# Attention scores computed by four row tiles of two heads instead of two row tiles of four heads, in a cross-attention and mixture-of-experts kernel

## The chip, the core and the metric

The kernel runs on one core of one Trainium2 chip. The metric is the device time of one execution in microseconds (us); lower is better. The core has TensorE (matrix products, written PE in the profile, its weight loads PEld), VectorE (DVE), ScalarE (ACT), GpSimd (POOL), and SyncE (SP), which issues most transfers. The engines run side by side, each takes its own instructions in order, and they meet by semaphores, which the kernel sets and waits for by hand.

## The reference, cut to what matters

All is f32. There are 4 sequences of 512 tokens of 256 features, and 64 context tokens for each sequence.

```
x1 = x + Wo( softmax( Q(layernorm(x)) K(ctx)^T / sqrt(16) ) V(ctx) ) + bo      # 16 heads of 16 features, 64 keys
gates = layernorm(x1) @ router_w + router_b ; the best 2 of 8 experts, softmax of their gates
out = x1 + mean over 2 shared experts of gelu(h @ sw1 + sb1) @ sw2 + sb2 + the 2 chosen experts, weighted
```

The change touches the term Q K^T alone: for each token 16 heads x 64 keys = 1024 scores.

## The kernel before

**Tiles and stages.** The 2048 tokens are 16 token tiles of 128 (NT = 16). Attention is a software pipeline over stages s. In one stage each engine works on several token tiles: the scores of tile s+1, maximum and shift of tile s, sums of tile s-1, transposes of tile s-2, values of tile s-3, output product of tile s-4, and the transposes of normalized rows of tile s-8. From stage 16 on, the products of the shared experts are interleaved with the rest of it (hidden products, line 1237, and output products, line 1143). After stage 47 come the routed experts. The order on each engine is written out by hand, and a wait holds up all that is behind it on its engine.

**What each engine issues in a stage of the attention.** Names are used below in this short form:

- TensorE: scores(s+1) (line 1084), then from s = 8 x2T(s-8) (line 1175), from s = 4 att(s-4) (line 1186), ot(s-3) (line 1198), tr(s-2) (eight transposes, line 1211), and in the odd stages 1 to 11 the query projection of two token tiles, q((s+3)/2) (line 1065).
- ScalarE: in the even stages QT, the copy of these queries from PSUM (line 549), then x2T(s-8) copy (line 600), OT(s-3) copy (line 607), exp(s) (line 612), rows(s-7) (line 618), PT(s-2) copy (line 624), and in stages 3 to 10 a copy of shared weights, s_hi (line 571). In stage 14 a copy xt_hi (line 577) follows.
- VectorE: max(s) (line 894, waits for scores(s)), shift(s) (line 903), in stages 0 to 8 statistics of x (lines 743 and 747), x1(s-4) (line 911, waits for att(s-4)), sum(s-1) (line 914, waits for exp(s-1)), statistics of x1 (line 920), reciprocal(s-1) (line 925).
- GpSimd: the product of the exponentials with the reciprocals (line 473), and small work.

**PSUM.** There are eight banks of 512 f32 columns. Scores have four, as two buffers of two banks (psS): token tile t takes buffer t % 2, and scores(t) waits until shift(t-2) has read its predecessor (line 1080). The bank psD serves q and att: att(s-4) waits until ScalarE has copied the queries out (qt_sb, line 1182), and q waits for x1 (line 1215). The bank psA serves x2T and ot: ot waits for the copy of x2T of the stage before (line 1194).

**Scores.** K is laid out as Kbd, block-diagonal: on the 64 partitions of a row tile lie 4 heads of 16 features, and each head has 64 columns of its own, zero on the partitions of the others. One product has 64 rows of Q (the stationary operand, 128 tokens) and 256 columns of Kbd. A token tile needs C = 2 chunks x RT = 2 row tiles = 4 products, which the trace shows as 8 instructions, since an f32 product is two instructions. The two row tiles write two different banks. Kbd is written by one VectorE product (batch 0, line 753) and HPR = 4 ScalarE copies (line 558), with masks that GpSimd makes (line 364).

Of the kernel before, what the change touches and what calls it, by code (L numbers as in the profile page):

```python
# [14 lines left out]
P = 128  # L15
# [4 lines left out]
L = 64  # L20
# [3 lines left out]
RT = 2  # L24
HPR = 4
# [87 lines left out]
def program(nc, ios, keep, scratch):  # L113
# [4 lines left out]
    with ExitStack() as es:  # L118
# [30 lines left out]
        psS = es.enter_context(nc.psum_tensor("psS", [P, 2, RT, 512], F32))  # L149
# [65 lines left out]
        def heads(t):  # L215

            return t.rearrange("p r (h k) -> p (r h) k", k=L)
# [127 lines left out]
        def _(pool):  # L345
# [18 lines left out]
            pool.tensor_tensor(out=maskK[:], in0=mask8[:, 0:HPR], in1=mask8[:, HPR:2 * HPR], op=ALU.add).then_inc(masks, 1)  # L364
# [173 lines left out]
        def _(act):  # L538
# [16 lines left out]
            act.wait_ge(masks, 11)  # L555
# [181 lines left out]
        def _(dve):  # L737
# [14 lines left out]
            dve.wait_ge(masks, 11)  # L752
# [137 lines left out]
            for s in range(FIRST_CHUNK + CHUNKS):  # L890
                if s < NT:
                    dve.wait_ge(scores_done, s + 1)
                    v = heads(psS[:, s % 2])
                    V.reduce_max(mx[:, s % 2], v, axis=AX.X).then_inc(max_done, 1)
# [4 lines left out]
                if s < NT:  # L899
                    if s >= NPR:  # L900
                        dve.wait_ge(pt_psum, s - NPR + 1)
                    dve.wait_ge(max_done, s + 1)
                    V.tensor_tensor(out=Pr[:, s % NPR], in0=v, in1=mx[:, s % 2].unsqueeze(2).to_broadcast([P, NH, L]),  # L903
                                    op=ALU.subtract).then_inc(shift_done, 1)
# [138 lines left out]
        def _(pe):  # L1043
# [25 lines left out]
            def scores(t):  # L1069
                b = t // TPB  # L1070
                if t == 0:
                    pe.wait_ge(q0_sb, 1)
                else:
                    pe.wait_ge(qt_sb, t // 2 + 1)
                if b == 0:
                    pe.wait_ge(k0_done, 1)
                else:
                    pe.wait_ge(k_done, HPR)
                if t >= 2:
                    pe.wait_ge(shift_done, t - 1)  # L1080
                for c in range(C):
                    for r in range(RT):
                        own = slice(r * L, (r + 1) * L)
                        last = T.matmul(psS[:, t % 2, r, c * HPR * L:(c + 1) * HPR * L], QT[own, t // 2 % 2, c, t % 2 * P:(t % 2 + 1) * P],  # L1084
                                        Kbd[own, c, b].rearrange("p h k -> p (h k)"), start=True, stop=True)
                last.then_inc(scores_done, 1)
# [9 lines left out]
            scores(0)  # L1096
            scores(1)
            queries(1)
            scores(2)

            pe.wait_ge(ld_wv, 16)
            for i, bank in enumerate((psA[:, :], psP[:, 1])):
                for b in range(2 * i, 2 * i + 2):
# [63 lines left out]
            for s in range(FIRST_CHUNK + CHUNKS):  # L1167
                if 2 <= s < NT - 1:
                    scores(s + 1)
# [7 lines left out]
                if 4 <= s < NT + 4:  # L1177
# [9 lines left out]
                    last.then_inc(att_psum, 1)  # L1187
                if 3 <= s < NT + 3:
# [6 lines left out]
                    for c in range(C):  # L1195
                        for j in range(TPB):
                            own = slice(CT * j, CT * (j + 1))
                            last = T.matmul(psA[own, D + c * P:D + (c + 1) * P], Vbd[:, t // TPB, c * P + CT * j:c * P + CT * (j + 1)],  # L1198
                                            PT[:, t % 2, 4 * (j // 2) + 2 * c + j % 2], start=True, stop=True)
# [23 lines left out]
                if 0 <= n < CHUNKS:  # L1223
                    q, e, k = n // CPG, n % CPG // HC, n % HC
                    if n == 0:
                        pe.wait_ge(shift_done, NT - 1)
# [143 lines left out]
def build(nc, a, out):  # L1370
    xg_d = nc.dram_tensor("xg_d", [XG_ROWS, ROW], F32, kind="Internal").ap()
    with ExitStack() as es:
# [13 lines left out]
        with ExitStack() as first:  # L1386
# [20 lines left out]
            Kbd, Vbd, QT = lay("Kbd", [P, C, B, HPR, L]), lay("Vbd", [P, B, D]), lay("QT", [P, 2, C, QT_TOK])  # L1407
            OT, WoT, bo_bc, sb2_bc = lay("OT", [P, 2, C, P]), lay("WoT", [P, C, D]), lay("bo_bc", [P, D]), lay("sb2_bc", [P, NSH, D])
# [63 lines left out]
```

## Time and profile before

| | us |
|---|---|
| median of 3 runs | 336.03 |
| the runs | 334.66, 340.51, 336.03 |
| the profiled execution | 332.25 |
| its span from first to last instruction | 330.5 |

| engine | busy share of the span |
|---|---|
| PE (matmul) | 93% |
| PEld (weight load) | 81% |
| DVE | 68% |
| ACT | 66% |
| POOL | 57% |

The trace is one execution. Times in its rows count from the start of its span. A row of the timeline gives start, duration, engine, line, operation, output<-input, shapes (partitions x elements) and count; a bracket at its end is the time that the engine sat idle before it, and what released it. Where several instructions are merged in a row (x8), the duration is from the first start to the last end; the next row can begin before that end, as matmuls are pipelined, so the time that a group takes from its engine is read from start to start.

### The profile page before, as it was taken

To read this page: it belongs to the slowest core of one execution; us is meant where nothing else is said; L and a number is where in the kernel's file an instruction comes from. 1 tells how busy PE (TensorE), PEld (TensorE's weight loads), DVE (VectorE), ACT (ScalarE), POOL (GpSimd) and SP (SyncE) were. 2 spreads that over 40 slices of the span, in tenths; PEclk is the share of its full clock that TensorE was granted. 3 is DMA by queue.
4 is the path that set the end of the run, shared out by engine and by line. 5 is a ranking of instruction groups with operands and counts; after the bars stand their busy time and mean duration, and the time that the engine had idled before them with its cause. 6 is when DMAs were issued, how large, how long until landed. Compare 5 with 4: busy or idle time off the path is not lost.

```text
span 330.5 us, 7676 instructions
## 1 busy us (share of the span) xinstructions
PE 307.7 (93%) x2390; PEld 269.0 (81%) x2390; DVE 225.2 (68%) x474; ACT 216.9 (66%) x438; POOL 189.0 (57%) x227
## 2 busy tenths in 40 slices
PE   3999999998899899999999999999999999999980
PEld 2767676676667787899999998989999999999970
DVE  0699999889815466688766546667687666667530
ACT  1365776777785886674855747667698678678540
POOL 5459889879943276676710071323355558557653
PEclk9999999999799999999999999999999999999995
DMA  7980000044000754245954704545447356544343
GB/s 245 401 330 2 3 0 3 0 129 177 16 18 1 269 195 147 97 153 143 319 192 127 216 8 119 93 71 93 65 83 97 64 99 98 74 57 52 47 52 44
DMA packets 27766, 36.32 MB, mean 110 GB/s; under 512 B 8368, under 2 KB 22064, under 8 KB 27344
## 3 DMA queue, kind: packets, MB, share of 16 engines
q1 hardware_dynamic: 19984, 25.02, 24.5%
q0 software_dynamic: 7456, 10.04, 17.8%
q10 hardware_dynamic: 288, 0.79, 0.8%
q8 instruction: 20, 0.33, 0.4%
q14 instruction: 18, 0.15, 0.2%
HBM read 22.64 MB, written 13.19 MB: 108 GB/s over the span
## 4 chain that ended last, share of the span: by engine, by line
PE 80%; ACT 6%; issue 4%; DVE 4%; DMA 3%; POOL 2%; SPq 0%; POOLq 0%; DVEq 0%; ACTq 0%
PE psS L1282 13%; PE psS L1237 12%; PE psP L1298 8%; PE psS L1143 4%; PE psP L1143 4%; PE psP L1302 4%; PE psD L1065 4%; PE psS L1329 4%; PE psS L1084 4%; PE psP L1211 3%; PE psP L1353 3%; PE psS L1146 2%; PE psP L1146 2%; PE psD L1186 2%; PE psA L1198 2%
## 5 line engine op out<-in xcount | busy, mean ns | idle before, releaser
L512 POOL DMA_INDIRECT out<-xres,meta x39 | 66.0, 1691 | 36.1 <-DMA out<-xres,meta 21.7
L936 DVE TENSOR_TENSOR h_lo<-g,h_hi 128x512 fp32r<-128x512 f32 x32 | 22.8, 713 | 33.8 <-ACT g L641 33.7
L640 ACT ACTIVATE h_hi<-psS,sb1T 128x512 fp32r<-128x512 f32 x32 | 22.0, 689 | 32.6 <-PE psS L1237 32.6
L473 POOL TENSOR_TENSOR Pr<-Pr,inv 128x1024 f32<-128x1024 f32 x16 | 31.3, 1956 | 11.5 <-DVE inv L925 11.5
L725 ACT ACTIVATE s_hi<-psS,b1c 128x256 fp32r<-128x256 f32 x60 | 25.6, 489 | 14.5 <-PE psS L1282 14.5
L1298 PE MATMUL psP<-w_lo,s_hi 128*128 x120 | 29.8, 281 | 0.0
L1298 PE MATMUL psP<-w_hi,s_hi 128*128 x120 | 29.7, 280 | 0.0
L1033 DVE TENSOR_TENSOR s_lo<-sraw,s_hi 128x512 fp32r<-128x512 f32 x30 | 20.6, 688 | 12.8 <-ACT sraw L728 12.8
L728 ACT ACTIVATE sraw<-psS,b1c 128x256 f32<-128x256 f32 x60 | 25.9, 502 | 0.0
L1237 PE MATMUL psS<-xt_hi,s_lo 128*128 128x512 f32 x64 | 25.4, 397 | 0.0
L1237 PE MATMUL psS<-xt_lo,s_hi 128*128 128x512 f32 x64 | 25.3, 395 | 0.0
L1237 PE MATMUL psS<-xt_hi,s_hi 128*128 128x512 f32 x64 | 25.0, 390 | 0.0
L1298 PEld LDWEIGHTS psP<-w_hi,s_hi 128*128 128x128 f32 x120 | 22.7, 189 | 0.0
L1298 PEld LDWEIGHTS psP<-w_lo,s_hi 128*128 128x128 f32 x120 | 22.7, 189 | 0.0
L641 ACT ACTIVATE g<-psS,sb1T 128x512 f32<-128x512 f32 x32 | 21.8, 682 | 0.0
L443 POOL DMA_INDIRECT xg_d<-rows_b,slots x16 | 18.4, 1153 | 5.9 <-issue 4.3
L443 POOL DMA_INDIRECT xg_d<-rows_a,slots x16 | 16.9, 1059 | 8.4 <-issue 4.3
L786 DVE TENSOR_TENSOR w_lo<-wraw,w_hi 128x512 fp32r<-128x512 f32 x32 | 20.9, 684 | 0.0
L503 POOL TENSOR_TENSOR s_free<-s_free,sbh 128x256 f32<-128x256 f32 x8 | 6.5, 849 | 25.0 <-DMA s_free<-in_b 25.0
L989 DVE SCALAR_TENSOR_TENSOR xres<-psP,meta,xres 128x256 f32<-128x256 f32 x26 | 12.6, 483 | 11.0 <-PE psP L1302 6.5
L903 DVE TENSOR_TENSOR Pr<-psS,mx 128x1024 f32<-128x1024 f32 x16 | 19.6, 1225 | 0.5
L1302 PE MATMUL psP<-w_hi,s_lo 128*128 x120 | 19.4, 284 | 0.0
(244 smaller groups left out, 1015.1 us busy)
## 6 DMA issues: line engine op xcount, KB each, us to landing
wraw<-in_w SPq DMA_DIRECT2D x16, 512.0 KB, 5.9
xg<-xg_d SPq DMA_DIRECT2D x15, 256.0 KB, 2.7
sraw<-in_sw SPq DMA_DIRECT2D x2, 1024.0 KB, 11.6
out<-xres SPq DMA_DIRECT2D x4, 512.0 KB, 3.2
xres<-in_x SPq DMA_DIRECT2D x3, 512.0 KB, 7.5
xTs<-in_xT SPq DMA_DIRECT2D x3, 512.0 KB, 8.4
xg<-xg_d SPq DMA_DIRECT2D x9, 128.0 KB, 2.1
xg_d<-filler SPq DMA_DIRECT2D x8, 130.0 KB, 2.2
```

Of the source, the lines that this page charges most:

```text
L443: pool.indirect_dma_start(xg_d, bass.IndirectOffsetOnAxis(ap=slots[:, k, t:t + 1], axis=0), row(t), None).then_inc(scattered[t // HALF_T][ ...
L473: pool.tensor_tensor(out=Pr[:, t % NPR], in0=Pr[:, t % NPR], in1=inv[:, t % 2].unsqueeze(2).to_broadcast([P, NH, L]), op=ALU.mult).then_in ...
L512: pool.indirect_dma_start(out, bass.IndirectOffsetOnAxis(ap=meta[:, n, 0:1].bitcast(U32), axis=0), y[:, n % NYB], None, compute_op=ALU.add ...
L640: A.activation(h_hi[:, n % 2], h_bank[n % 2], ACT.Gelu, bias=bias).then_inc(hhi_done, 1)
L725: ins = A.activation(hp_hi[:, i % 2, k], hp_bank[i % 2][k], ACT.Gelu, bias=b1c[:, i % 2, k:k + 1])
L728: ins = A.activation(gp[:, i % 2, k], hp_bank[i % 2][k], ACT.Gelu, bias=b1c[:, i % 2, k:k + 1])
L936: V.tensor_tensor(out=h_lo[:, n % 2], in0=g[:, n % 2], in1=h_hi[:, n % 2].bitcast(F32), op=ALU.subtract).then_inc(hlo_done, 1)
L1143: T.matmul(y_bank[u], h_hi[:, m % 2, u * P:(u + 1) * P], b[:, e, wc], start=(m % CPG == 0 and i == 0), stop=False)
L1237: last = T.matmul(h_bank[n % 2], a[:, e, wc], b[:, q % 2, c], start=(i == 0), stop=(i == 3 * C - 1))
L1282: last = T.matmul(hp_bank[i % 2][k], a[i % 2][:, c * HF + k * P:c * HF + (k + 1) * P], b[:, i % 2, c * PT_TOK:(c + 1) * PT_TOK], start=(m ...
L1298: T.matmul(res_bank[n % 2], hp_hi[:, i % 2, c, own], b[:, bass.ds(e, 1), C * HF + c * D:C * HF + (c + 1) * D].squeeze(1), start=(c == 0 an ...
L1302: last = T.matmul(res_bank[n % 2], hp_lo[:, i % 2, c, own], w_hi[:, bass.ds(e, 1), C * HF + c * D:C * HF + (c + 1) * D].squeeze(1), start= ...
```

## The change

Scores are computed by RT = 4 row tiles of HPR = 2 heads. A row tile has 32 partitions, a product has 32 rows and 128 columns, and a token tile needs 2 chunks x 4 row tiles = 8 products, 16 instructions. Each row tile writes a bank of its own, so a token tile takes columns 0 to 255 of all four psS banks, and the next takes columns 256 to 511 of the same four. As both now lie in the same banks, scores(t) waits for shift(t-1) instead of shift(t-2). scores(s+1) is moved behind x2T(s-8) and att(s-4) in a stage, and at the start the first query projection is put ahead of scores(1), and scores(2) between the two value projections. VectorE reads four banks (256 columns of each) instead of two (all 512). Kbd has half as many columns, its ScalarE copies are two instead of four, and the mask takes one more small GpSimd sum. The heads end up in another order in Pr, so ot picks other slices of PT. The first hidden product waits for shift(15) instead of shift(14). A filler keeps the SBUF addresses behind Kbd as they were.

```diff
-RT = 2
-HPR = 4
+RT = 4
+HPR = 2
...
-        psS = es.enter_context(nc.psum_tensor("psS", [P, 2, RT, 512], F32))
+        psS = es.enter_context(nc.psum_tensor("psS", [P, 2, 2, 512], F32))
...
+        def score_cols(t):
+            first = t % 2 * C * HPR * L
+            return psS[:].rearrange("p a r n -> p (a r) n")[:, :, first:first + C * HPR * L]
...
-            pool.tensor_tensor(out=maskK[:], in0=mask8[:, 0:HPR], in1=mask8[:, HPR:2 * HPR], op=ALU.add).then_inc(masks, 1)
+            pool.tensor_tensor(out=mask8[:, 0:4], in0=mask8[:, 0:4], in1=mask8[:, 4:8], op=ALU.add).then_inc(masks, 1)
+            pool.wait_ge(masks, 11)
+            pool.tensor_tensor(out=maskK[:], in0=mask8[:, 0:2], in1=mask8[:, 2:4], op=ALU.add).then_inc(masks, 1)
...
-                    v = heads(psS[:, s % 2])
-                    V.reduce_max(mx[:, s % 2], v, axis=AX.X).then_inc(max_done, 1)
+                    v = score_cols(s).rearrange("p r (h k) -> p r h k", k=L)
+                    V.reduce_max(per_bank(mx[:, s % 2]), v, axis=AX.X).then_inc(max_done, 1)
...
-                if t >= 2:
-                    pe.wait_ge(shift_done, t - 1)
+                if t >= 1:
+                    pe.wait_ge(shift_done, t)
                 for c in range(C):
                     for r in range(RT):
-                        own = slice(r * L, (r + 1) * L)
-                        last = T.matmul(psS[:, t % 2, r, c * HPR * L:(c + 1) * HPR * L], QT[own, t // 2 % 2, c, t % 2 * P:(t % 2 + 1) * P],
+                        own = slice(r * CT, (r + 1) * CT)
+                        last = T.matmul(score_cols(t)[:, r, c * HPR * L:(c + 1) * HPR * L], QT[own, t // 2 % 2, c, t % 2 * P:(t % 2 + 1) * P],
                                         Kbd[own, c, b].rearrange("p h k -> p (h k)"), start=True, stop=True)
...
             scores(0)
+            queries(1)
             scores(1)
-            queries(1)
-            scores(2)
-
             pe.wait_ge(ld_wv, 16)
             for i, bank in enumerate((psA[:, :], psP[:, 1])):
+                if i == 1:
+                    scores(2)
...
             for s in range(FIRST_CHUNK + CHUNKS):
-                if 2 <= s < NT - 1:
-                    scores(s + 1)
                 for t in x2T_at(s):
...
                         last = T.matmul(psD[:, 0:D], OT[:, t % 2, c], WoT[:, c], start=(c == 0), stop=(c == C - 1))
                     last.then_inc(att_psum, 1)
+                if 2 <= s < NT - 1:
+                    scores(s + 1)
                 if 3 <= s < NT + 3:
...
-                        pe.wait_ge(shift_done, NT - 1)
+                        pe.wait_ge(shift_done, NT)
```

## Rows read from the trace of the kernel before

**Rows 1.** The page: busy time by engine; the granted TensorE clock in 40 slices.
```profile
PE 307.7 (93%) x2390; PEld 269.0 (81%) x2390; DVE 225.2 (68%) x474; ACT 216.9 (66%) x438; POOL 189.0 (57%) x227
...
PEclk9999999999799999999999999999999999999995
```

**Rows 2.** Timeline of VectorE: shifts and x1 additions of stages 3 to 15.
```profile
26.18 1.23 DVE L903 TENSOR_TENSOR Pr<-psS,mx 128x1024 f32<-128x1024 f32 x1
...
35.40 1.23 DVE L903 TENSOR_TENSOR Pr<-psS,mx 128x1024 f32<-128x1024 f32 x1
...
44.89 1.23 DVE L903 TENSOR_TENSOR Pr<-psS,mx 128x1024 f32<-128x1024 f32 x1
...
51.15 0.42 DVE L911 TENSOR_TENSOR xres<-psD,xres 128x256 f32<-128x256 f32 x1
...
54.44 1.23 DVE L903 TENSOR_TENSOR Pr<-psS,mx 128x1024 f32<-128x1024 f32 x1
...
61.28 0.42 DVE L911 TENSOR_TENSOR xres<-psD,xres 128x256 f32<-128x256 f32 x1 [1.27 <-PE psD L1186]
...
64.50 1.23 DVE L903 TENSOR_TENSOR Pr<-psS,mx 128x1024 f32<-128x1024 f32 x1
...
71.38 0.42 DVE L911 TENSOR_TENSOR xres<-psD,xres 128x256 f32<-128x256 f32 x1 [1.30 <-PE psD L1186]
...
74.59 1.23 DVE L903 TENSOR_TENSOR Pr<-psS,mx 128x1024 f32<-128x1024 f32 x1
...
83.30 1.23 DVE L903 TENSOR_TENSOR Pr<-psS,mx 128x1024 f32<-128x1024 f32 x1
```

**Rows 3.** Timeline of TensorE: stage 7's queries, stage 8, start of stage 9.
```profile
46.82 1.99 PE L1065 MATMUL psD<-xTs,WqT 128*128 128x256 f32 x8
48.75 1.13 PE L1084 MATMUL psS<-Kbd,QT 64*128 64x256 f32 x8
49.81 0.44 PE L1175 MATMUL psA<-ident,rows_a 128*128 128x128 f32 x2
50.09 1.03 PE L1186 MATMUL psD<-WoT,OT 128*128 128x256 f32 x4
51.05 0.64 PE L1198 MATMUL psA<-PT,Vbd 128*32 128x128 f32 x16
51.62 1.09 PE L1211 MATMUL psP<-ident,Pr 128*128 128x128 f32 x8
52.64 1.13 PE L1084 MATMUL psS<-Kbd,QT 64*128 64x256 f32 x8
```

**Rows 4.** Timeline of ScalarE: stage 7, and the query copy of stage 8.
```profile
45.82 0.39 ACT L607 ACTIVATE OT<-psA 128x256 f32<-128x256 f32 x1 [0.87 <-PE psA L1198]
46.15 1.15 ACT L612 ACTIVATE Pr<-Pr,rs 128x1024 f32<-128x1024 f32 x1
47.20 0.59 ACT L618 ACTIVATE rows_a<-xres,nmr,rs 128x256 f32<-128x256 f32 x1
47.69 1.00 ACT L624 ACTIVATE PT<-psP 128x1024 f32<-128x1024 f32 x1
48.60 0.62 ACT L571 ACTIVATE s_hi<-sraw 128x512 fp32r<-128x512 f32 x1
49.12 0.58 ACT L549 ACTIVATE QT<-psD 128x512 f32<-128x512 f32 x1
```

**Rows 5.** Timeline of VectorE: stage 0 and the first maximum of stage 1.
```profile
13.20 1.22 DVE L894 TENSOR_REDUCE mx<-psS 128x16 f32<-128x1024 f32 x1 [0.58 <-PE psS L1084]
14.45 1.22 DVE L903 TENSOR_TENSOR Pr<-psS,mx 128x1024 f32<-128x1024 f32 x1
...
16.14 1.19 DVE L894 TENSOR_REDUCE mx<-psS 128x16 f32<-128x1024 f32 x1
```

**Rows 6.** Timeline of TensorE: transposes tr(13) and tr(14).
```profile
84.96 1.97 PE L1211 MATMUL psP<-ident,Pr 128*128 128x128 f32 x8
...
89.35 1.09 PE L1211 MATMUL psP<-ident,Pr 128*128 128x128 f32 x8
```

More of the change, by code:

```diff
@@ L213, in stats_of, with per_bank @@
             return range(*stats_at[s:s + 2]) if s + 1 < len(stats_at) else ()
-        def heads(t):
-            return t.rearrange("p r (h k) -> p (r h) k", k=L)
+        def score_cols(t):
+            first = t % 2 * C * HPR * L
+            return psS[:].rearrange("p a r n -> p (a r) n")[:, :, first:first + C * HPR * L]
+        def per_bank(t):
+            return t.rearrange("p (r h) -> p r h", r=RT)
         def w_cols(t, k):
@@ L554, in _ @@
             act.wait_ge(k0_done, 1)
-            act.wait_ge(masks, 11)
+            act.wait_ge(masks, 12)
             kt = psP[:, 0].rearrange("p (f b k) -> p f b k", f=C, k=L)
@@ L751, in _ @@
             dve.wait_ge(k_psum, 1)
-            dve.wait_ge(masks, 11)
+            dve.wait_ge(masks, 12)
             V.tensor_tensor(out=Kbd[:, :, 0], in0=psP[:, 0].rearrange("p (f b k) -> p f b k", f=C, k=L)[:, :, 0].unsqueeze(2).to_broadcast([P, C, HPR, L]),
@@ L902, in _ @@
                     dve.wait_ge(max_done, s + 1)
-                    V.tensor_tensor(out=Pr[:, s % NPR], in0=v, in1=mx[:, s % 2].unsqueeze(2).to_broadcast([P, NH, L]),
+                    V.tensor_tensor(out=Pr[:, s % NPR].rearrange("p (r h) k -> p r h k", r=RT), in0=v,
+                                    in1=per_bank(mx[:, s % 2]).unsqueeze(3).to_broadcast([P, RT, NH // RT, L]),
                                     op=ALU.subtract).then_inc(shift_done, 1)
@@ L1198, in _ @@
                             last = T.matmul(psA[own, D + c * P:D + (c + 1) * P], Vbd[:, t // TPB, c * P + CT * j:c * P + CT * (j + 1)],
-                                            PT[:, t % 2, 4 * (j // 2) + 2 * c + j % 2], start=True, stop=True)
+                                            PT[:, t % 2, 2 * j + c], start=True, stop=True)
                     last.then_inc(ot_psum, 1)
@@ L1407, in build @@
             Kbd, Vbd, QT = lay("Kbd", [P, C, B, HPR, L]), lay("Vbd", [P, B, D]), lay("QT", [P, 2, C, QT_TOK])
+            fit(2 * WPE, Kbd, Vbd, QT)
             OT, WoT, bo_bc, sb2_bc = lay("OT", [P, 2, C, P]), lay("WoT", [P, C, D]), lay("bo_bc", [P, D]), lay("sb2_bc", [P, NSH, D])
```

## The prediction

> **What bounds the kernel now.** I read the page first. TensorE is busy most of the time and its granted clock is full but for one slice [rows 1]. That average invites "fewer TensorE cycles, less time", so I looked at which wait ends last in the attention, by the timelines of three engines. VectorE's timeline [rows 2] shows the surprise: between the shifts it waits for TensorE only twice, 1.27 and 1.30 us, in stages 10 and 12, which follow stages with a query projection. Else it works without a break and sets the pace: shift(5) to shift(7) is 9.49 us and shift(13) to shift(15) 8.71, two stages of 4.75 and of 4.35. TensorE's timeline [rows 3] shows why both look full. Start to start, queries take 1.93, scores 1.06, x2T 0.28, att 0.96, ot 0.57, tr 1.02: 3.89 us without queries and 5.82 with, 9.7 a pair. What lets it pass the long stage is its lead: scores(9) start at 48.75, while shift(8) ends near 50.9, midway between shift(7)'s end at 46.12 and shift(9)'s at 55.67. The second score buffer is what allows this.
>
> **What the change removes.** TensorE time in scores. From rows 3: eight products of 256 columns one after the other take 1.93 (queries), the same eight in pairs on two row tiles 1.06. So a wave of 256 columns costs (1.93 - 1.06) / 4 = 0.22, and 1.06 - 4 x 0.22 = 0.18 to 0.19 is fixed. After the change there are four waves of four tiles with 128 columns: 4 x 0.11 + 0.19 = 0.63. I take 0.65, done 0.07 later, as 1.13 is to 1.06. The bounds are ot, also sixteen instructions of 128 columns in four waves, but with narrower weights, 0.57 [rows 3], and no gain at all, 1.06. TensorE gains 0.41 a token tile, 6.6 us in all. The Trainium skill (TensorE: Matmul & The Clock Gate, Part 3) gives 3.07x for four row tiles; by it 1.93 would become 0.63, the same sum.
>
> **What it adds: a wait.** scores(s+1) needs the end of shift(s), which I call T(s), instead of shift(s-1). VectorE's own next need of scores(s+1) is over 2 us after T(s), and scores need 0.7: that part is hidden. But behind scores on TensorE stand ot, tr and the queries, and behind ot stands ScalarE's whole stage, as OT(s-3) comes before exp(s) in its order. At its end stands QT, and att(s-3), which is ahead of scores(s+2), waits for QT because they share psD. In stage 7 now ot(4) is long done and exp(7) starts at 46.15, 0.03 after T(7) = 44.89 + 1.23 = 46.12 [rows 2, 4]. After, the chain from T(s) to x1(s-3) for s = 7 and 9 is, with 0.04 for a handover:
>
> scores 0.04 + 0.65; ot 0.64; OT copy 0.04 + 0.33; exp 1.05; rows 0.49; PT 0.91; s_hi 0.52; QT 0.58; att 0.04 + 1.03; x1 0.04. Sum 6.36 us [rows 3, 4].
>
> Stages 3 and 5 have no rows: 5.87. Stage 11 has no s_hi: 5.84. Before, the same distance was 51.15 - 46.12 = 5.03 for s = 7 (VectorE never idle) and 5.61 and 5.65 for s = 9 and 11, the two stalls included [rows 2]. From x1 to the next shift's end is VectorE alone: 55.67 - 51.15 = 4.52, and without statistics 65.73 - 61.28 = 4.45. So from odd shift to odd shift, with T(3) = 27.41, T(5) = 36.63, T(7) = 46.12, T(9) = 55.67, T(11) = 65.73, T(13) = 75.82, T(15) = 84.53 [rows 2]:
>
> - 3 to 5: 5.87 + 4.52 = 10.39, was 9.22: +1.17
> - 5 to 7: 10.39, was 9.49: +0.90
> - 7 to 9: 6.36 + 4.52 = 10.88, was 9.55: +1.33
> - 9 to 11: 6.36 + 4.45 = 10.81, was 10.06: +0.75
> - 11 to 13: 5.84 + 4.45 = 10.29, was 10.09: +0.20
> - 13 to 15, no queries: att now stands behind x2T, which stands behind rows and exp: 0.69 + 0.64 + 0.37 + 1.05 + 0.59 + 0.04 + 0.28 + 1.03 + 0.04 = 4.73, + 4.45 = 9.18, was 8.71: +0.47
>
> Sum +4.82. **Start:** scores(0) are done 0.41 sooner (max(0) at 12.79 instead of 13.20), but max(1) now needs shift(0), 0.72 of scores and two handovers: 15.26 + 0.80 = 16.06, was 16.14 [rows 5]: -0.08. **End:** tr(14) came 89.35 - 84.53 = 4.82 after T(15) [rows 2, 6]. After, from T(14): scores(15) to PT as above (0.69, 0.64, 0.37, 1.05, 0.49, 0.91), the xt_hi copy (as large as PT, 0.91), the x2T copy (0.33, as OT) and a handover: 5.43, which is 0.84 after T(15); then ot 0.64, OT 0.37, exp 1.05, rows 0.63, x2T 0.28, att 0.96, ot 0.57: 5.34. +0.52. Everything behind is a chain of the same engines and goes along. Sum: -0.08 + 4.82 + 0.52 = **+5.3 us**.
>
> **At nothing:** the smaller Kbd (its product and copies end before anything waits for them, since TensorE is on the first queries; two ScalarE copies, each shorter than QT's 0.58, are spared; they run beside stage 0, and if they were in the way it would be a gain of 1 us); the extra mask sum (a tile of 128x2, due long before stage 0 at 13.20; uncovered it would cost less than x1's 0.42, for 128x256); shift(15) instead of shift(14) before the first hidden product, which stands behind tr(14), 4.8 us after shift(15) already; the filler in SBUF. VectorE's maxima and shifts read as many elements, from four banks instead of two; no row has that pattern, so it is bounded by 0 and by 0.05 on each of 32 instructions, the spread of the maxima shown (1.19 to 1.22) rounded up: 1.6 us. I take 0.
>
> **Rivals.** *The relief decides* (other side): if TensorE's lead isn't what carries it and the chain from T(s) stays under the 5.03 and 5.6 us of now, the stalls of 1.27 and 1.30 and the start's 0.08 go: -2.7, 333.4. It decides at the att of stages 10 and 12. For it: these are the only waits for TensorE in the stretch. Against: the chain needs QT at ScalarE's end. *ScalarE isn't in the way*: if QT follows the queries at once, the chain is TensorE's own: 0.69 + 0.57 + 1.02 + 1.93 + 0.28 + 0.04 + 1.03 + 0.04 = 5.60 in stages 7 to 11, 5.32 before; the pairs then give +0.62, +0.35, +0.57, -0.01 and -0.04, with the start +1.4: 337.4. Against: QT is behind four copies by the order. *The clock falls*: in one slice now it is lower, and tr(13) took 1.97 instead of 1.09 [rows 1, 6], right where scores are missing from the stage. After, TensorE has 8.9 us of work in 10.9 of a pair, less than now. Each chain that it hits has scores, ot and att (2.3 us) twice as long; three hits are +7, 348. The Trainium skill (TensorE: Matmul & The Clock Gate, Part 1) says that the clock is granted by recent activity, which agrees with that slice and speaks against sparser work. *The tiles don't overlap* (the change doesn't do what it says): if the weight loads of four tiles of 128 columns queue, sixteen take as tr does, 1.02 / 8 each, 2.0 us; with 1.35 more in each of six pairs, and as much again where even stages then bind too, that is +8 to +16, up to 352. Against: pairs and fours do overlap [rows 3]. The same skill (Part 2, LDWEIGHTS) says that a load of 32 rows takes as long as one of 128; that alone changes nothing if they go side by side.
>
> **How the numbers follow.** The sum is against the profiled execution: 332.25 + 5.3 = 337.6. The median of the runs is 3.8 above it; I carry the difference over: 336.0 + 5.3 = **341.3 us**. Scores at 0.57 give about 0.5 less, at 0.85 some 2.5 more (1.2 in the pairs, the rest where even stages begin to bind). Chances: forecast 0.64, ScalarE not in the way 0.10, relief 0.12, clock 0.08, tiles 0.06. A measurement of this kernel can't tell 2% (6.7 us) from no change. Faster by more would need over twice VectorE's stalls for TensorE; 0.07, mostly from the runs' spread of 5.9 us. Slower by more: clock and tiles, 0.14, and a third of the forecast's 0.64, as +5.3 is near 6.7: 0.35. Same: 0.58. The range, 335 to 348, takes in scores of 0.57 to 0.85, the bound on VectorE, ScalarE's rival at 337.4, the spread of the runs around each, and the lighter clock cases; it leaves out relief, the tiles and the rest of the clock, some 0.2.
>
> **What would show it.** Right: score groups of 16 in about 0.65; each starting within 0.1 of a shift's end; the exponential some 1.7 after the shift instead of 0.03; VectorE idle before x1 in stages 4, 6, 8, 10 and 12, 0.9 to 2.1 each, about 7 in all instead of 2.6, and 0.4 in 14; shift(15) starting near 88. Wrong: VectorE's stalls unchanged or gone, scores over 0.9, maxima slower than 1.2, or lower clock in the slices of the attention.

## The result and the profile after

The changed kernel is slower. Median of six runs 344.17 us (341.81 to 345.83); the kernel before, in the same six rounds, 338.18 (334.66 to 341.07). The ratio is 1.0254 with a 95% interval of 1.0181 to 1.0327; it is above that of the medians, 1.018, because runs of the kernel before that lay over 1.5% above its fastest are left out as disturbed. Timed again on another chip, it was 340.83 against 332.25, ratio 1.029 [1.0239, 1.034]. So the change costs 6 to 9 us; I had forecast 5.3 and a time of 341.3, with 0.58 for "same" within 2% and 0.35 for slower. The profiled execution took 341.81, span 340.1, against 332.25 and 330.5.

The 9.6 us between these two spans lie in four stretches. Up to the first maximum the trace after is 1.0 shorter (12.18 against 13.20), from there to the last maximum 8.2 longer (77.02 against 68.84), from there to the first hidden product 0.7 longer (8.86 against 8.17), and behind it 1.7 longer (242.0 against 240.3). The forecast is about the second and third.

The page after: TensorE is less busy, 301.7 us instead of 307.7 [rows 1], in a longer span, and the low slice of the clock has moved from slice 11 to slice 5, into the attention's long chains. My list of signs had low clock in the slices of the attention among those of being wrong.

```profile
PE 301.7 (89%) x2518; PEld 266.7 (78%) x2518; DVE 226.2 (67%) x474; ACT 215.1 (63%) x436; POOL 188.5 (55%) x228
...
PEclk9999799999999999999999999999999999999995
```

VectorE's timeline after (the additions x1 that it waited for, and shifts 5, 7 and 9), to be held against [rows 2]:

```profile
33.04 0.42 DVE L919 TENSOR_TENSOR xres<-psD,xres 128x256 f32<-128x256 f32 x1 [1.33 <-PE psD L1192]
...
36.32 1.23 DVE L910 TENSOR_TENSOR Pr<-psS,mx 128x1024 f32<-128x1024 f32 x1
...
45.30 0.43 DVE L919 TENSOR_TENSOR xres<-psD,xres 128x256 f32<-128x256 f32 x1 [2.67 <-PE psD L1192]
...
48.58 1.22 DVE L910 TENSOR_TENSOR Pr<-psS,mx 128x1024 f32<-128x1024 f32 x1
...
56.38 0.43 DVE L919 TENSOR_TENSOR xres<-psD,xres 128x256 f32<-128x256 f32 x1 [1.50 <-PE psD L1192]
...
59.67 1.23 DVE L910 TENSOR_TENSOR Pr<-psS,mx 128x1024 f32<-128x1024 f32 x1
...
67.47 0.42 DVE L919 TENSOR_TENSOR xres<-psD,xres 128x256 f32<-128x256 f32 x1 [2.08 <-PE psD L1192]
...
77.98 0.42 DVE L919 TENSOR_TENSOR xres<-psD,xres 128x256 f32<-128x256 f32 x1 [1.51 <-PE psD L1192]
...
87.25 0.42 DVE L919 TENSOR_TENSOR xres<-psD,xres 128x256 f32<-128x256 f32 x1 [0.26 <-PE psD L1192]
```

Where it waited twice, it now waits behind every query projection: 1.33, 2.67, 1.50, 2.08 and 1.51, 9.1 us instead of 2.57. One of the five, 2.67, is larger than the chain explains; in a second trace of the same kernel it is 1.02, and the five are 7.4, where I had said about 7. Experiment e6 turns to it.

TensorE's timeline after, stage 7 from scores(8) to stage 8:

```profile
49.95 0.73 PE L1092 MATMUL psS<-Kbd,QT 32*128 32x128 f32 x16 [1.57 <-DVE Pr L910]
50.61 0.64 PE L1206 MATMUL psA<-PT,Vbd 128*32 128x128 f32 x16
51.18 1.09 PE L1219 MATMUL psP<-ident,Pr 128*128 128x128 f32 x8
52.11 1.89 PE L1073 MATMUL psD<-xTs,WqT 128*128 128x256 f32 x8
53.84 0.38 PE L1181 MATMUL psA<-ident,rows_a 128*128 128x128 f32 x2
55.24 1.10 PE L1192 MATMUL psD<-WoT,OT 128*128 128x256 f32 x4 [1.02 <-issue]
```

Scores take 0.66 from start to start (50.61 - 49.95), 0.65 forecast, 1.06 before [rows 3]. But TensorE stands still for 1.57 us until the shift is done, then again for 1.02 before the output product. ScalarE's timeline of the same stage says what that second wait is for:

```profile
51.32 0.38 ACT L614 ACTIVATE OT<-psA 128x256 f32<-128x256 f32 x1 [1.91 <-PE psA L1206]
51.60 1.14 ACT L619 ACTIVATE Pr<-Pr,rs 128x1024 f32<-128x1024 f32 x1
52.64 0.59 ACT L625 ACTIVATE rows_a<-xres,nmr,rs 128x256 f32<-128x256 f32 x1
53.13 1.01 ACT L631 ACTIVATE PT<-psP 128x1024 f32<-128x1024 f32 x1
54.03 0.62 ACT L578 ACTIVATE s_hi<-sraw 128x512 fp32r<-128x512 f32 x1
54.55 0.59 ACT L556 ACTIVATE QT<-psD 128x512 f32<-128x512 f32 x1
```

Shift(7) ended at 48.58 + 1.22 = 49.80. The exponential starts 1.80 later instead of 0.03 [rows 4], the query copy ends at 55.14, the product starts at 55.24. From the shift's end to x1 it is 56.38 - 49.80 = 6.58; forecast 6.36, before 5.03.

### The profile page after: what moved, and what is told of

The parts are those of the page before. It is cut to its first block, busy times and chain, and to the rows that moved or that the text cites. A ratio compares the mean times of both kernels' runs of the same rounds, so it can differ in the third digit from the quotient of the medians.

```text
span 340.1 us, 7931 instructions
## 1 busy us (share of the span) xinstructions
PE 301.7 (89%) x2518; PEld 266.7 (78%) x2518; DVE 226.2 (67%) x474; ACT 215.1 (63%) x436; POOL 188.5 (55%) x228
## 4 chain that ended last, share of the span: by engine, by line
PE 70%; ACT 9%; DVE 8%; issue 5%; DMA 3%; POOL 2%; another core or an unknown queue 1%; POOLq 0%; SPq 0%; DVEq 0%; ACTq 0%
PE psS L1290 12%; PE psS L1245 10%; PE psP L1306 7%; PE psS L1337 4%; PE psP L1310 4%; PE psS L1151 4%; PE psP L1151 4%; PE psD L1192 3%; PE psD L1073 3%; PE psA L1206 3%; PE psP L1361 3%; PE psS L1092 2%; POOL out L519 2%; PE psP L1219 2%; PE psS L1154 2%
## 5 line engine op out<-in xcount | busy, mean ns | idle before, releaser
L519 POOL DMA_INDIRECT out<-xres,meta x39 | 65.1, 1669 | 37.2 <-DMA out<-xres,meta 24.8
L647 ACT ACTIVATE h_hi<-psS,sb1T 128x512 fp32r<-128x512 f32 x32 | 22.0, 688 | 32.1 <-PE psS L1245 26.8
L614 ACT ACTIVATE OT<-psA 128x256 f32<-128x256 f32 x16 | 6.2, 384 | 27.2 <-PE psA L1206 27.2
L1192 PE MATMUL psD<-WoT,OT 128*128 128x256 f32 x64 | 16.8, 385 | 4.1 <-issue 3.3
```

The costliest lines, as they stand in the source:

```text
L519: pool.indirect_dma_start(out, bass.IndirectOffsetOnAxis(ap=meta[:, n, 0:1].bitcast(U32), axis=0), y[:, n % NYB], None, compute_op=ALU.add ...
L647: A.activation(h_hi[:, n % 2], h_bank[n % 2], ACT.Gelu, bias=bias).then_inc(hhi_done, 1)
L1192: last = T.matmul(psD[:, 0:D], OT[:, t % 2, c], WoT[:, c], start=(c == 0), stop=(c == C - 1))
```

## The experiments

To compare kernels without what happens ahead of and behind the attention, I use one number of each trace, the time from the first maximum (stage 0) to the last (stage 15), and the periods between maxima. All are starts of the maxima in the timeline (the last digit can differ by 0.01 from rounded rows). A low clock is a stretch in which the trace has a granted clock of 0.5; the column gives where it starts and how long it is. Times are medians; "before" is the kernel before in the same rounds on the same chip.

```
                                            us     before   ratio [95%]             max0-max15  low clock in attention
before (first trace)                                                                  68.84     84.3, 3.4 us (in stage 15)
changed kernel, first trace               344.17  338.18  1.0254 [1.0181, 1.0327]     77.02     39.1, 3.4 us
changed kernel, again (after_again)       340.83  332.25  1.029  [1.0239, 1.034]      75.36     91.8, 3.4 us
e1 wait alone                             366.56  332.01  1.103  [1.0987, 1.1073]    104.07     six, 24 us in all
e5 order alone                            337.88  332.25  1.0173 [1.0152, 1.0194]     73.55     none
e2 wait + order, two tiles                344.01  332.01  1.0362 [1.0323, 1.0402]     78.94     none
e4 cheap scores, nothing else             331.01  332.01  0.9972 [0.9954, 0.9989]     68.20     none
e3 changed + exp first                    339.41  332.01  1.0211 [1.0163, 1.0258]     76.62     27.1, 6.8 us
e6 changed + filler                       338.50  332.25  1.0209 [1.0175, 1.0243]     75.35     none
e7 changed + exp first + filler           335.91  332.25  1.0114 [1.009, 1.0137]      73.77     none
e8 e7 + queries first                     340.10  334.40  1.0148 [1.0093, 1.0204]     73.11     none
e11 e8 with less filler                   338.26  336.54  1.0128 [1.0003, 1.0253]     71.87     none
e9 before + exp first                     336.91  334.40  1.0083 [1.0021, 1.0146]     68.20     none
e10 e9 + filler in stage 15               337.64  334.40  1.0045 [0.9976, 1.0114]     68.22     none

periods between maxima, stages 0-1, 1-2, ..., 14-15:
before       2.95 4.44 4.40 4.41 4.74 4.74 4.75 4.74 4.81 4.35 5.71 4.35 5.75 4.35 4.35
after        3.42 4.47 4.41 4.41 6.17 4.74 7.52 4.74 6.35 4.50 6.52 4.57 5.95 4.57 4.70
after_again  3.42 4.47 4.41 4.41 6.17 4.74 5.86 4.74 6.35 4.50 6.52 4.56 5.96 4.56 4.70
e1           4.36 6.10 5.33 4.47 6.89 8.24 6.89 8.77 7.06 8.63 7.00 6.99 7.00 7.77 8.57
e5           2.99 4.47 4.41 4.41 4.74 4.75 4.75 4.74 5.52 4.91 6.73 4.97 6.23 4.97 4.97
e2           3.80 4.47 4.41 4.41 6.58 4.74 6.27 4.74 6.75 4.91 6.73 4.97 6.23 4.97 4.97
e3           3.42 4.47 4.41 4.40 9.03 4.74 5.84 4.74 5.84 4.35 6.17 4.35 6.17 4.35 4.35
e6           3.42 4.47 4.41 4.41 6.17 4.74 5.86 4.74 6.35 4.50 6.52 4.56 5.95 4.56 4.69
e7           3.41 4.47 4.41 4.40 6.15 4.74 5.84 4.74 5.84 4.35 6.17 4.35 6.17 4.35 4.36
e8           3.42 4.47 4.40 4.41 6.16 4.74 5.51 4.74 5.73 4.35 6.06 4.35 6.06 4.35 4.36
e11          3.41 4.47 4.41 4.40 6.15 4.74 5.07 4.74 5.47 4.35 5.80 4.35 5.80 4.35 4.36
e4           2.95 4.44 4.41 4.40 4.74 4.74 4.74 4.74 4.75 4.35 5.57 4.35 5.32 4.35 4.35
e9           2.95 4.44 4.41 4.40 4.74 4.74 4.74 4.74 4.87 4.35 5.60 4.35 5.17 4.35 4.35
```

The theories: **chain** (the scores now start at a shift's end, and what stands behind them on TensorE and ScalarE arrives late for VectorE), **relief** (TensorE's busy time decides) and **clock** (a TensorE with pauses is granted less clock).

**e1, the wait alone.** The kernel before with

```diff
-                if t >= 2:
-                    pe.wait_ge(shift_done, t - 1)
+                if t >= 1:
+                    pe.wait_ge(shift_done, t)
```

> The kernel before with one line changed: scores(t) waits for shift(t-1) instead of shift(t-2); two row tiles, order and banks as before. Chain theory (a lost lead behind the shift costs the time): scores now stand ahead of x2T, att, ot and the rest of the stage on TensorE, and VectorE needs att right after the shift, so after each shift's end it waits for scores (1.06) and then att (1.0): periods of 6.6 to 6.8 us from stage 4 on instead of 4.35 to 4.75, in sum 22 to 25 us slower than before. Clock theory (what costs is that a sparser TensorE is granted less clock): TensorE has as much work as before, so little more than the few us of single waits, under 8 us. Relief theory (TensorE's busy time decides): no change beyond 2 us.

It took 366.56 us, 34.5 more than before (ratio 1.103). Relief can't be the whole account: TensorE has exactly the work of the kernel before. TensorE's timeline in stage 7 and the start of stage 8:

```profile
51.26 1.14 PE L1084 MATMUL psS<-Kbd,QT 64*128 64x256 f32 x8 [1.14 <-DVE Pr L903]
52.33 1.13 PE L1186 MATMUL psD<-WoT,OT 128*128 128x256 f32 x4
53.39 0.64 PE L1198 MATMUL psA<-PT,Vbd 128*32 128x128 f32 x16
53.96 1.09 PE L1211 MATMUL psP<-ident,Pr 128*128 128x128 f32 x8
58.15 2.08 PE L1084 MATMUL psS<-Kbd,QT 64*128 64x256 f32 x8 [3.09 <-DVE Pr L903]
60.15 2.07 PE L1186 MATMUL psD<-WoT,OT 128*128 128x256 f32 x4
```

The wait goes round: TensorE waits for the shift, VectorE for the output product behind the scores. The periods of 6.89 to 7.06 are what the chain gives. Those of 7.8 to 8.8 fall into stretches in which the granted clock is halved (0.50 from 57.3 to 64.1); the last two rows show the same products in 2.1 us instead of 1.1. So the clock, which I had as a rival, has a share as well. The five long periods are 7.2 us above their neighbours of 6.9 to 7.0, and one more low stretch, at 16.3, lies in the start. That leaves some 27 of the 35.2 us between first and last maximum to the chain, more than the 22 to 25 that I expected.

**e5, the order alone.** The kernel before with scores(s+1) behind x2T and att, both buffers and the old wait kept.

```diff
-                if 2 <= s < NT - 1:
-                    scores(s + 1)
                 for t in x2T_at(s):
...
                     last.then_inc(att_psum, 1)
+                if 2 <= s < NT - 1:
+                    scores(s + 1)
```

> The kernel before with scores(s+1) behind x2T and att (and the start's order), both score buffers and the wait for shift(t-2) kept, two row tiles. Chain theory: the lead is given up by the order too, since scores(s+1) now stand behind att(s-4), which waits for the query copy: 4 to 6 us slower than before, 12 less than the wait and order together at most; periods 4.7 to 4.8 until stage 7 and 6.2 to 6.7 behind the queries of stages 7 to 11. If the wait on the shift alone made the loss, no slower than before by more than 1 us.

5.6 us slower than before, as the chain says. The order gives up the lead too, since scores then stand behind att, which waits for the query copy. It does so from stage 8 on alone (5.52, 6.73, 6.23 behind queries); until then the periods are those of before. From stage 8 on scores also stand behind x2T. Where no queries came just before, TensorE sits idle 1.0 us ahead of x2T for the rows from ScalarE, and those periods are 4.91 to 4.97 instead of 4.35.

**e2, wait and order without the four tiles.** e1's and e5's edits together.

> The kernel before with the wait and the order of the changed kernel, but still two row tiles of four heads: the change without its tiles. Chain theory: each chain from a shift's end has 0.41 us more of scores than in the changed kernel, and the stages without queries begin to bind too: 4 to 6 us slower than the changed kernel, 10 to 13 slower than before. Periods after query stages 6.2 to 6.7, others 4.7 to 5.0. Relief theory: 16 x 0.41 = 6.6 us slower than the changed kernel. Clock theory: TensorE is busier than in the changed kernel, so fewer low stretches, and not slower than it.

344.01 us, 12.0 more than before. From first to last maximum 78.94, 10.1 more than before and 3.6 more than the changed kernel without a low clock there (75.36), where I expected 4 to 6 against the changed kernel. So the four tiles do what they are for: wait and order cost 10.1 there, and with the tiles 6.5 is left. The tiles give 3.6 back, not the 16 x 0.41 = 6.6 of TensorE time that they spare. The periods between stages 2 and 3 and 3 and 4, where nothing waits for scores, are the same in all kernels of the table but e1.

**e4, cheap scores and nothing else.** The kernel before, with 128 of 256 columns from token tile 2 on; half of the scores then keep older values.

```diff
+                        n = HPR if t < 2 else HPR // 2
-                        last = T.matmul(psS[:, t % 2, r, c * HPR * L:(c + 1) * HPR * L], QT[...],
-                                        Kbd[own, c, b].rearrange("p h k -> p (h k)"), start=True, stop=True)
+                        last = T.matmul(psS[:, t % 2, r, c * HPR * L:(c * HPR + n) * L], QT[...],
+                                        Kbd[own, c, b, 0:n].rearrange("p h k -> p (h k)"), start=True, stop=True)
```

> The kernel before, with both buffers and its order, but from token tile 2 on only the first two heads of each product are computed (128 columns instead of 256; the other half of the score columns keeps older values): what cheaper scores are worth where no wait is added. Scores then take about 0.6 us instead of 1.06. Chain theory: VectorE waits for TensorE only in stages 10 and 12; these two waits shrink by 0.4 to 0.9 each, 1 to 1.5 us faster than before, less than can be measured. Relief theory: 3 us or more faster. The rest of the kernel is the same.

1.0 us faster, ratio 0.9972 [0.9954, 0.9989]. Its scores take 0.64 from start to start, so TensorE has 14 x 0.42 = 5.9 us less to do, and this 1.0 is all that it is worth where VectorE sets the pace. The relief theory, with 3 us or more, is out. Its two waits are still there, smaller than in [rows 2]:

```profile
61.46 0.42 DVE L911 TENSOR_TENSOR xres<-psD,xres 128x256 f32<-128x256 f32 x1 [1.12 <-PE psD L1187]
71.13 0.42 DVE L911 TENSOR_TENSOR xres<-psD,xres 128x256 f32<-128x256 f32 x1 [0.88 <-PE psD L1187]
```

**e3, exp first.** The changed kernel with two blocks of ScalarE exchanged.

```diff
                 if 3 <= s < NT + 3:
-                    ...  OT(s-3) copy
                 if s < NT:
                     ...  exp(s)
+                if 3 <= s < NT + 3:
+                    ...  OT(s-3) copy
```

> The changed kernel with ScalarE's exp(s) ahead of its OT(s-3) copy. TensorE's work and waits are the same. Chain theory: exp starts at the shift's end instead of 1.7 us after it, and what stands behind it (rows, PT, s_hi, query copy) 1.05 us sooner; the chain of stages 7 and 9 is then bound by the queries and their copy (5.9 instead of 6.4), those of stages 3, 5 and 11 stay at 5.9, and the stages without queries lose their stall of 0.2 to 0.4: 1.5 to 2.5 us faster than the changed kernel, visible in the trace as periods of 4.3 instead of 4.6 from stage 12 on. Clock theory: no difference beyond where the low stretches fall. If ScalarE's order was the whole of it, 4 us or more.

The periods behind the queries of stages 7 and 9 fell from 6.35 and 6.52 to 5.84 and 6.17, those without queries from 4.5 to 4.7 to 4.35. One period was 9.03 instead of 6.2. In time it is 7.4 us slower than before, the changed kernel 8.6 in other rounds on another chip, so a gain of 1.5 to 2.5 isn't shown by the times. TensorE's timeline around it, the scores that waited for shift(3) and what followed:

```profile
24.03 1.10 PE L1219 MATMUL psP<-ident,Pr 128*128 128x128 f32 x8
27.72 1.24 PE L1092 MATMUL psS<-Kbd,QT 32*128 32x128 f32 x16 [2.60 <-DVE Pr L910]
28.89 1.08 PE L1206 MATMUL psA<-PT,Vbd 128*32 128x128 f32 x16
29.90 1.97 PE L1219 MATMUL psP<-ident,Pr 128*128 128x128 f32 x8
31.66 2.99 PE L1073 MATMUL psD<-xTs,WqT 128*128 128x256 f32 x8
```

The same groups take 0.73, 0.64, 1.09 and 1.89 at full clock. The granted clock was 0.5 for 6.8 us from 27.1 on. That began in a pause of 2.60 us and lay across the longest period of the kernel.

**after_again and e6, the filler.** So I timed the changed kernel again, and beside it with small products of the identity with itself at the heads of stages 3 to 15, into a part of psA that nothing reads then, as many as fit the pauses.

```diff
+            fill = {3: 8, 5: 4, 7: 4, 4: 2, 6: 2, 8: 2, 10: 2, 12: 2, 9: 3, 11: 3, 13: 3, 14: 3, 15: 3}
             for s in range(FIRST_CHUNK + CHUNKS):
+                if s in fill:
+                    ...  waits for the copies out of psA
+                    for _ in range(fill[s]):
+                        T.matmul(psA[:, 0:P], ident[:], ident[:], start=True, stop=True)
```

> The changed kernel once more, on the chip and beside the runs of this group. Chain theory plus clock: about 6 us slower than before by the chains, and 1 to 3 us more where a stretch of low granted clock falls into the attention; where that stretch falls may differ from the first trace (39 us), and the one long period moves with it.

> The changed kernel with 2 to 8 small products of the identity with itself at the head of stages 3 to 15 on TensorE, in the time in which it would wait, into a PSUM region that nothing reads; results and waits as before. Clock theory: the granted clock stays full in the attention, no period of 7.5 us or more, and the median is 1 to 2 us below the changed kernel's, its runs closer together. Chain theory alone: within 0.5 us of the changed kernel, as the filler fits the waits; where it doesn't fit it costs up to 0.3 a stage.

With filler the median is 338.50 against 340.83 in the same rounds, 2.3 us less with useless work added. These are four runs each, 337.82 to 339.81 and 339.74 to 343.18, and the intervals of their ratios just touch, so the size is uncertain. No low stretch is left in the attention. The page of e6, where the changed kernel had a low slice:

```profile
PEclk9999999999999999999999999999999999999995
```

TensorE's timeline of stages 2 and 3 in e6, with the filler (L1183) in the pause:

```profile
22.95 1.09 PE L1227 MATMUL psP<-ident,Pr 128*128 128x128 f32 x8
23.88 1.95 PE L1183 MATMUL psA<-ident 128*128 128x128 f32 x16
26.65 0.73 PE L1092 MATMUL psS<-Kbd,QT 32*128 32x128 f32 x16 [0.82 <-DVE Pr L910]
```

Period by period e6 equals after_again to 0.01, so its filler delays nothing. In the first trace of the changed kernel the stretch cost 7.52 - 5.86 = 1.66 us between stages 6 and 7. In after_again it came at 91.8 us, behind the last maximum, where it cost some 0.5 before the first hidden product (9.40 from the last maximum, against 8.86 in the first trace and in e6). So these two traces alone don't show 2.3 us of clock: their spans differ by 1.7, of which 1.1 lie ahead of the first maximum (12.87 and 11.79), where the filler can't act.

The clocks of all runs go with it, though. The granted clock, averaged over a whole execution, was 0.976 to 0.987 in all ten runs of the changed kernel and 0.979 to 0.985 in the four of e3, but 0.989 to 0.991 in those of e6 and 0.989 to 0.993 in those of e7. In after_again the two runs at 0.982 took 343.18 and 341.91, those at 0.985 and 0.987 took 339.74 and 339.76.

The Trainium skill (TensorE: Matmul & The Clock Gate, Part 1) says that activity releases the throttle. The traces agree as far as they go: in the first trace and in e3 the stretch follows a pause of 1.57 us or begins in one of 2.60, in e1 each of the six begins in or within 1.5 us after a pause of 2.2 to 3.1, and none of the four traces with filler in the pauses (e6, e7, e8, e11) has one in the attention. But the same pauses also pass without one (after_again, e2), and the stretches at 84.3 of the kernel before and at 91.8 of after_again follow pauses of no more than 1.0. What decides whether a pause is followed by one isn't shown.

**e7, exp first with filler.** e3's and e6's edits together.

> The changed kernel with exp(s) ahead of the OT copy on ScalarE and the filler of the run before. Chain and clock together: chains as without filler (periods of 5.8 to 6.2 behind queries, 4.35 to 4.75 else), no low stretch in the attention, about 3 us faster than the changed kernel and some 4 to 5 slower than the kernel before. If the long period of 9.0 us in the trace without filler came from the order and not from the clock, it stays.

335.91, 2.6 less than e6 and 3.7 more than before (ratio 1.0114 [1.009, 1.0137]). 73.77 - 68.84 = 4.9 of the chain's cost are left. The period of 9.03 is gone (6.15), so it was the clock. ScalarE's timeline of stage 7 shows what binds now: the query copy waits for the queries, 0.19 us.

```profile
48.58 1.15 ACT L613 ACTIVATE Pr<-Pr,rs 128x1024 f32<-128x1024 f32 x1 [0.75 <-DVE Pr L910]
50.06 0.38 ACT L619 ACTIVATE OT<-psA 128x256 f32<-128x256 f32 x1 [0.33 <-PE psA L1214]
50.34 0.59 ACT L625 ACTIVATE rows_a<-xres,nmr,rs 128x256 f32<-128x256 f32 x1
51.05 1.02 ACT L631 ACTIVATE PT<-psP 128x1024 f32<-128x1024 f32 x1
51.98 0.62 ACT L578 ACTIVATE s_hi<-sraw 128x512 fp32r<-128x512 f32 x1
52.78 0.60 ACT L556 ACTIVATE QT<-psD 128x512 f32<-128x512 f32 x1 [0.19 <-PE psD L1073]
```

**e8 and e11, queries first.** e7 with the queries of stages 5 to 11 right behind scores on TensorE, and their copy right behind exp on ScalarE. e11 leaves out the filler of stages 6, 8, 10 and 12.

```diff
                     scores(s + 1)
+                if s % 2 == 1 and s >= 5 and (s + 3) // 2 < NPAIR:
+                    pe.wait_ge(x1_done, s - 3)
+                    queries((s + 3) // 2)
                 if 3 <= s < NT + 3:
```

> The kernel of the run before (changed kernel, exp first, filler) with the query projections of stages 5 to 11 ahead of ot and tr on TensorE, right behind scores, and their copy right behind exp on ScalarE. Chain theory: the longest piece of the chain from a shift's end to the output product was scores, ot, tr, queries, query copy; without ot and tr (1.6 us) TensorE's own work of the stage decides, 5.0 to 5.4 behind stages 5 and 7 and 5.6 behind 9 and 11 instead of 5.8 and 6.2, so 2 us faster than that run and within 1 to 2 us of the kernel before. If TensorE's sum of work alone set those periods, no change.

Only 0.66 us less than e7 between the maxima, where I expected 2. TensorE's timeline of e8, from scores(8) to the output product before x1 at 53.56:

```profile
47.75 0.73 PE L1094 MATMUL psS<-Kbd,QT 32*128 32x128 f32 x16 [0.68 <-DVE Pr L912]
48.40 1.99 PE L1075 MATMUL psD<-xTs,WqT 128*128 128x256 f32 x8
50.33 0.64 PE L1219 MATMUL psA<-PT,Vbd 128*32 128x128 f32 x16
50.90 1.09 PE L1232 MATMUL psP<-ident,Pr 128*128 128x128 f32 x8
51.83 0.61 PE L1185 MATMUL psA<-ident 128*128 128x128 f32 x4
52.28 0.38 PE L1191 MATMUL psA<-ident,rows_a 128*128 128x128 f32 x2
52.50 1.03 PE L1202 MATMUL psD<-WoT,OT 128*128 128x256 f32 x4
```

No pause is left in it, and my own filler (L1185), which had filled pauses in e7, now lies in TensorE's chain: 0.65 + 1.93 + 0.57 + 0.93 + 0.45 (filler) + 0.22 + 1.03 + 0.04 = 5.82.

```diff
-            fill = {3: 8, 5: 4, 7: 4, 4: 2, 6: 2, 8: 2, 10: 2, 12: 2, 9: 3, 11: 3, 13: 3, 14: 3, 15: 3}
+            fill = {3: 8, 5: 4, 7: 4, 4: 2, 9: 3, 11: 3, 13: 3, 14: 3, 15: 3}
```

> The kernel e8 without the filler at the heads of stages 6, 8, 10 and 12 (there TensorE no longer waits, and the 0.45 us of filler lay in its chain). Chain theory: those four periods fall by 0.4 each, from 5.51, 5.73, 6.06 and 6.06 to about 5.1, 5.3, 5.65 and 5.65; first to last maximum 71.5 us instead of 73.1 (kernel before: 68.8). In time 2.5 to 3.5 us slower than the kernel before, unless the stretch behind the attention is disturbed on the chip. If the chain was bound by something else, periods as in e8.

71.87 (71.5 expected), periods 5.07, 5.47, 5.80, 5.80: the first fell by 0.44 as expected, the others by 0.26 instead of 0.4. So the filler was part of the cause. The two kernels' times say less than their traces: the ratios are 1.0148 and 1.0128 [1.0003, 1.0253], and on these two chips the runs of the kernel before spread from 332.5 to 341.4. By the ratios both are slower than before, and neither is shown to be faster than e7.

**e9 and e10, a better kernel before.** The kernel before with ScalarE's exchange of e3, and with that and filler in stage 15.

```diff
                 if s < NT:
                     ...  exp(s)
+                if 3 <= s < NT + 3:
+                    ...  OT(s-3) copy, which stood ahead of exp(s)
 ...
+                if s == 15:                                   # e10 alone
+                    ...  waits for the copies out of psA
+                    for _ in range(3):
+                        T.matmul(psA[:, 0:P], ident[:], ident[:], start=True, stop=True)
```

> The kernel before (two row tiles, two buffers, old order) with exp(s) ahead of the OT copy on ScalarE. There exp started at the shift's end already except where TensorE was late; chain theory: only the two waits of VectorE in stages 10 and 12 shrink by 0.3 to 0.5 each, some 0.7 us faster than before, 0.2%.

> As the run before, with three small filler products at the head of stage 15 on TensorE, where the kernel before had a stretch of low granted clock at 84 us in its trace. If that stretch costs something there, up to 1 us faster than the run without; as tr(14) waits for GpSimd there, more likely 0 to 0.3. Likely the fastest kernel of the study, 1 us below the kernel before.

Between the maxima both are 0.6 us shorter than before (68.20, 68.22), as forecast. Their times are not: 1.0083 [1.0021, 1.0146] and 1.0045 [0.9976, 1.0114]. In e9's trace the first maximum came at 14.97, 1.8 later than in that of before, though nothing ahead of it was changed (12.89 in e10). And both lose 3.7 and 6.4 us behind the first hidden product, in the shared experts, where ScalarE sits idle. The waits of e9 from 105 to 200 us (who waited for what, total, times, longest):

```profile
ACT h_hi L640 <- remote: 4.3, 3, 2.6
ACT gT L645 <- remote: 2.8, 1, 2.8
```

The first trace of the changed kernel has such waits too (L647 is the same operation), in the same stretch:

```profile
ACT h_hi L647 <- remote: 4.3, 2, 3.6
ACT gT L652 <- remote: 2.7, 1, 2.7
```

Those of e10 add up to 13.8 us, the longest 7.4; e8 and e11 have them too, 9.2 and 4.7. The traces of before, after_again and e1 to e7 have none. From the first hidden product to the end it takes 244.0 us in e9, 242.0 in the first trace after, 246.7 in e10, 245.3 in e8 and 242.7 in e11, in the traces without such waits 240.0 to 240.3, but for e1's 241.9. Always among these waits is that of gT, a copy of finished products: 2.75 to 2.9 in each of the five, and nothing in the other nine traces. What the profile calls remote I can't say. No experiment settles whether e9 is the faster kernel; nothing here beats the kernel before by a measured time, save e4, which leaves half of the scores out.

## Why the prediction came out as it did

**The bound (right).** VectorE sets the pace and TensorE's relief is hidden: e4 gives 1.0 us for 5.9 of it. The rival of relief is out.

**The scores' cost (right).** 0.65 forecast, 0.66 measured, nothing of it lost to queueing weight loads. The rival of tiles that don't overlap is out. The Trainium skill (TensorE: Matmul & The Clock Gate, Part 3) has its 3.07x for products of 512 columns; the estimate of 0.63 from it is borne out here for 128 columns, by 1.93 / 0.66 = 2.9.

**The chain from the shift's end (right in its links, 0.2 short each).** VectorE waited in stages 4, 6, 8, 10 and 12, and 0.26 in 14. The exponential came 1.80 after the shift instead of 1.7. From the shift's end to x1 it was 6.14, 6.09, 6.58, 6.58 and 6.07 in after_again for stages 3 to 11, where I had 5.87, 5.87, 6.36, 6.36 and 5.84. So each pair of stages was 0.2 longer than my 10.39, 10.39, 10.88, 10.81 and 10.29 (10.58, 10.60, 11.09, 11.02, 10.52 in after_again, e.g. 4.41 + 6.17), and the last 9.26 instead of 9.18: 1.1 us in sum. The term of the sum that was too small is the handover. I took 0.04 from an engine that was nearly busy; TensorE, idle before, starts scores 0.15 after the shift's end and att 0.10 after the copy's, and that att takes 1.10 instead of 1.03.

**Start and end (0.15 and 0.2 short).** From max(0) to max(1) 3.42 instead of 3.27. From the last maximum to tr(14) it was 8.01 (97.21 - 89.20), before 7.32 (89.35 - 82.03) [rows 6]: +0.69 for my +0.52.

**The sum (near, in part by luck).** +5.3 forecast. Without low clock and remote waits, e6 against the kernel before says +6.5 to the last maximum (75.35 - 68.84), less 0.4 as max(0) itself comes sooner, and 0.7 at the end: 6.8. Measured on one chip in the same rounds: 6.25 for e6, 8.6 for the changed kernel. The 2.3 between them I put down to the clock; the mean clock of the runs goes with it, but what a stretch costs is shown for three traces alone (0.5, 1.66 and 2.9). And the 6.0 between the first medians is near 5.3 because the kernel before had 338.18 in these six rounds and not the 336.03 that I started from; by the ratio the same rounds give 8.5. By class, slower was less likely to me than same: chain and handover already come to about 2%, and the clock goes on top.

**The clock (a rival with 0.08, which came true beside the forecast).** This is the step that failed: I made low clock an alternative to the chain and left it out of the sum, at nothing, when it came together with the chain. In two of three traces of the new chain without filler (after, e3) a low stretch fell between the maxima and cost 1.66 and 2.9 us (9.03 - 6.15), in e1 six of them. I had priced a hit at 2.3, which is in between, and three hits; there was one. I had compared shares of busy time, 8.9 in 10.9 against 9.7 in 10.06; the traces point rather to TensorE's pauses for the shift, up to 3.1 us in e1 with its six stretches, up to 2.6 in the changed kernel and up to 1.8 in e2 with none, but no run varies their length alone. The mean clocks suggest that it struck in all ten runs of the changed kernel (at most 0.987) and in one of the four of e2 (0.980, the others 0.990); whether in the attention or behind it, only the traces tell.

**"ScalarE isn't in the way" (priced wrong).** I gave 5.60 and 5.32 for TensorE's own chain from the shift's end to x1, and left out the query copy behind the queries. e7 shows it: with ScalarE out of the way the same distance stays at 6.07 to 6.12 for stages 3 to 11, as the copy waits for the queries. So TensorE and ScalarE bound stages 3, 5 and 11 nearly alike, and only 7 and 9 were ScalarE's.

**What I had not separated: wait and order.** I put the loss down to the wait. By the first-to-last maxima the order alone costs 4.7, the wait alone 35.2 (with low clock), both 10.1, and with four tiles 6.5. Given the wait, the new order is what saves the kernel from most of its cost; without the wait, the order is a loss of its own.

**VectorE reading four banks (right at nothing).** Maxima took 1.16 to 1.23, shifts 1.22 to 1.23, in both kernels.

## What to carry to other kernels

A double buffer given up for a faster producer turns the producer from "ahead" to "after the consumer": price it by the chain of everything that stands behind the producer on its engine, and on the engines that this feeds, not by the producer's own time. Where two engines look fully busy, ask which one sets the pace and which one's lead carries the other; 5.9 us taken off TensorE were worth 1.0 here. Halving the work alone, as in e4, tells this before a layout is changed. And a TensorE that gets regular pauses can lose clock on top. A few products into a free part of PSUM in the pauses kept the clock full in the attention here, and the median fell by 2.3 us; with the pauses gone they lay in the way (e8).

## What the runs showed of the hardware

- Four row tiles of 32 rows with 128 columns, sixteen instructions into four banks: 0.66 us from start to start, against 1.06 for eight instructions of 256 columns on two row tiles [rows 3].
- After a pause TensorE's group starts 0.10 to 0.15 us after its releaser ended, and four instructions of 256 columns take 1.10 instead of 1.03 in the trace of the changed kernel.
- At the lower clock level (granted 0.5, 1.2 instead of 2.4 GHz), groups took 1.7 to 1.8 times as long: transposes 1.97 for 1.09, scores 1.24 for 0.73, att 2.07 for 1.13. A stretch of 3.4 us cost 1.7 us (first trace after), one of 6.8 us 2.9 (e3), where they fell into the chain.
- In five of fourteen traces ScalarE sat idle in waits that the profile calls remote, in the stretch of the shared experts, 4.7 to 13.8 us in all and up to 7.4 at a time. These executions took 1.7 to 6.4 us longer behind the first hidden product than the 240.3 of the kernel before, as much as the edits of this study. The cause is open.
